# Adding a state's products on TensorE in two pieces instead of one, in the scan layers of a four-layer sequence model

## The reference

```
xz = h @ in_w;  xs, z = split(xz);  xs = silu(xs)
proj = xs @ xproj_w
dt = softplus(proj[..., :512] + dt_bias);  Bm, Cm = the next 64 and 64 columns
step:  hst = hst * exp(dt_t * A) + (dt_t * x_t) * B_t      # 512 channels x 64 states
       y_t = einsum('bds,bs->bd', hst, C_t)                # the sum over the states
y = ys + xs * Dskip
out = (y * silu(z)) @ out_w
```

## Time and profile before

| | |
|---|---|
| median of 3 runs | 4470.44 us (4468.05 to 4472.06) |
| the profiled execution | 4466.95 us |
| its span on the core | 4465.1 us |
| mean granted TensorE clock | 0.984 of full speed |
| scans of layer 1 | 295.0 to 1638 us |
| scans of layer 3 | 1948.7 to 4415.9 us |

### The profile page before, as it was taken

The page is one execution under the profiler, slowest core; times in us unless marked ns, Lnnn a source line. Parts: engine busy times, 40 slices in busy tenths (PEclk is TensorE's granted clock), DMA queues, the critical chain, the costliest instruction groups (busy, mean ns, idle before and its releaser), DMA issues.

```text
span 4465.1 us, 109964 instructions
## 1 busy us (share of the span) xinstructions
PE 4170.5 (93%) x45790; PEld 3234.7 (72%) x45790; DVE 4010.6 (90%) x3859; ACT 3863.4 (87%) x6050; POOL 3622.6 (81%) x1328
## 2 busy tenths in 40 slices
PE   9999899899899988989999999999999999999998
PEld 5457677677677764457877777778777777777777
DVE  6669999999999976669999999999999999999996
ACT  4569899899899964579999999999999999999995
POOL 3338898898888973349989998999998999888995
PEclk8999999999999999999999999999999999999999
DMA  4012121222122221032242422422422422323221
GB/s 167 1 29 67 58 65 62 57 60 67 58 59 67 69 73 41 1 53 72 85 78 79 86 70 76 83 74 82 84 75 68 87 82 94 62 79 70 72 83 40
DMA packets 241500, 305.18 MB, mean 68 GB/s; under 512 B 116448, under 2 KB 175712, under 8 KB 241008
## 3 DMA queue, kind: packets, MB, share of 16 engines
q1 hardware_dynamic: 241008, 298.15, 24.5%
HBM read 289.84 MB, written 8.26 MB: 67 GB/s over the span
## 4 chain that ended last, share of the span: by engine, by line
PE 41%; ACT 35%; DVE 16%; issue 7%; POOL 1%; DVEq 0%; DMA 0%; SPq 0%; POOLq 0%; ACTq 0%
PE psum L863 10%; ACT weights_c L1800 10%; PE psum L1152 8%; DVE work L2316 8%; PE psum L1134 8%; PE psum L1131 7%; ACT work L1817 6%; ACT work L1800 6%; ACT weights_c L1817 5%; PE psum L1279 5%; DVE weights_c L2316 4%; ACT L1498 2%; ACT modulation L1800 1%; PE psum L1362 1%; PE psum L1075 1%
## 5 line engine op out<-in xcount | busy, mean ns | idle before, releaser
L2739 POOL TENSOR_TENSOR work<-work,weights_a 128x2048 f32<-128x2048 f32 x512 | 1975.5, 3869 | 152.2 <-DVE work L2316 116.1
L2316 DVE TENSOR_TENSOR_SCAN work<-weights_c,psum 128x512 f32<-128x512 f32 x1316 | 1507.9, 1202 | 84.8 <-PE psum L1134 74.5
L2739 POOL TENSOR_TENSOR weights_c<-weights_c,weights_a 128x2048 f32<-128x2048 f32 x256 | 988.8, 3869 | 54.3 <-DVE weights_c L2316 52.8
L1134 PE MATMUL psum<-ident,work 128*128 128x128 f32 x5464 | 934.0, 273 | 0.0
L1800 ACT ACTIVATE work<-work,decay 128x504 f32<-128x504 f32 x1172 | 816.1, 707 | 72.0 <-DVE weights_c L2316 34.7
L2316 DVE TENSOR_TENSOR_SCAN weights_c<-work,psum 128x512 f32<-128x512 f32 x586 | 677.0, 1200 | 29.2 <-PE psum L1134 28.0
L2316 DVE TENSOR_TENSOR_SCAN work<-work,psum 128x512 f32<-128x512 f32 x586 | 675.7, 1200 | 28.5 <-PE psum L1134 26.8
L1134 PE MATMUL psum<-ident,weights_c 128*128 128x128 f32 x3752 | 696.9, 276 | 0.0
L1134 PEld LDWEIGHTS psum<-ident,work 128*128 128x128 f32 x5464 | 668.9, 142 | 0.0
L1152 PE MATMUL psum<-ident,work 64*128 64x64 f32 x16800 | 658.3, 229 | 10.2 <-POOL work L2739 8.1
L1152 PEld LDWEIGHTS psum<-ident,work 64*128 64x128 f32 x16800 | 586.0, 140 | 99.2 <-issue 74.4
(11 more groups left out here) (221 smaller groups left out, 6464.7 us busy)
## 6 DMA issues: line engine op xcount, KB each, us to landing
weights_a<-c_rows SPq DMA_DIRECT2D x384, 512.0 KB, 3.7
work<-b_diagonals SPq DMA_DIRECT2D x240, 128.0 KB, 2.2
weights_c<-b_diagonals SPq DMA_DIRECT2D x112, 128.0 KB, 2.1
b_diagonals<-weights_c SPq DMA_DIRECT2D x1, 4096.0 KB, 18.3
weights_c<-in_L_cond_fwd_in_w SPq DMA_DIRECT2D x8, 512.0 KB, 5.6
weights_c<-in_L_cond_fwd_xproj_w SPq DMA_DIRECT2D x4, 1024.0 KB, 7.2
weights_c<-in_L_cond_bwd_in_w SPq DMA_DIRECT2D x8, 512.0 KB, 5.4
weights_c<-in_L_cond_bwd_xproj_w SPq DMA_DIRECT2D x4, 1024.0 KB, 7.2
```

The source lines that it names most:

```text
L1134: last = nc.tensor.transpose(PS[:, bank, t * P:(t + 1) * P], buf["scaled"][s % INPUTS][t][:, j * P:(j + 1) * P], IDENT[:, :])
L2316: v.tensor_tensor_scan(buf["ring"][s % RING][:, along, j], buf["decay"][q % DECAYS[l]][:, along], PS[:, 4 + q % LOOKAHEAD, along], 0.0, AL ...
L2739: g.tensor_tensor(state, state, row.unsqueeze(2).broadcast_to([P, T, DC]), ALU.mult).then_inc(ss["prod_ready"], 1)
```

## The change

The add of a state is cut in two. Its turns 0 and 1 (16 transposes) come at PE's step 4s+9, and turns 2 and 3 (16 more) at step 4s+11. For the first state of a sum, these are 4s+11 and 4s+13. The wait for `half_turned` is now one wait at the second piece, for a semaphore that the first piece raised two steps earlier; the waits of `prod_ready`, `sum_done` of the state before, and of the first state's banks stand at the first piece. `sum_done` is raised by the second piece, at 4s+11 instead of 4s+10.

A piece of a projection or of another job that is due at a step which holds an add piece waits for the next step. Since adds are now at the odd steps, jobs go to the even ones. The skip term's add moves from step 22 (66) to 23 (67), stays in one place, and counts two increments of `skip_added` instead of one, for which the waits of ACT are adapted.

The instructions of DVE, ACT, POOL and SP stand in the same order as before.

```diff
-            step = s * DC + (11 if s % (states * together) == 0 else 10)
-            self.adds.setdefault(step, []).append(s)
+            step = s * DC + (11 if s % (states * together) == 0 else 9)
+            for half in range(2):
+                self.adds.setdefault(step + 2 * half, []).append((s, half))
...
-SKIPS = {1: (22, 66), 3: (22, 22)}
+SKIPS = {1: (23, 67), 3: (23, 23)}
...
-                def turn_by_rows(flat, begins, ends):
-
-                    nonlocal turns_done
-                    half, before = P // 2, turns_done
-                    for turn in range(TT):
-                        if turn >= 2:
-                            pe.wait_ge(ss["half_turned"], before + turn - 1)
+                def turn_by_rows(flat, turns, begins, ends):
+
+                    half = P // 2
+                    for turn in turns:
...
-                def add_up(s):
+                def add_up(s, half):
...
+                    flat = buf["ring"][s % RING].rearrange("p t j -> p (t j)")
+                    if half:
+                        pe.wait_ge(ss["half_turned"], s + 1)
+                        turn_by_rows(flat, (2, 3), begins, ends).then_inc(ss["sum_done"], 1)
+                        return
...
-                    turn_by_rows(flat, begins, ends).then_inc(ss["sum_done"], 1)
+                    turn_by_rows(flat, (0, 1), begins, ends).then_inc(ss["half_turned"], 1)
...
-                    for s in pl.adds.get(q, ()):
-                        add_up(s)
+                    for s, half in pl.adds.get(q, ()):
+                        add_up(s, half)
...
-                        while at is not None and (at <= step or step == pl.steps - 1):
+                        while at is not None and (at <= step and q not in pl.adds or step == pl.steps - 1):
```

More of the change, by code:

```diff
@@ L1136, in scan_input @@
                     last.then_inc(ss["input_ready"], 1)
-                turns_done = 0
-                def turn_by_rows(flat, begins, ends):
-                    nonlocal turns_done
-                    half, before = P // 2, turns_done
-                    for turn in range(TT):
-                        if turn >= 2:
-                            pe.wait_ge(ss["half_turned"], before + turn - 1)
+                def turn_by_rows(flat, turns, begins, ends):
+                    half = P // 2
+                    for turn in turns:
                         for k in range(DC):
@@ L1156, in turn_by_rows @@
                                                         tile_position=(g * half, 0))
-                        if turn < 2:
-                            last.then_inc(ss["half_turned"], 1)
-                            turns_done += 1
                     return last
-                def add_up(s):
+                def add_up(s, half):
                     r, n = divmod(s, pl.states)
                     begins, ends = s % (pl.states * pl.together) == 0, (s + 1) % (pl.states * pl.together) == 0
+                    flat = buf["ring"][s % RING].rearrange("p t j -> p (t j)")
[3 more added lines that the diff above has]
+                        return
                     if begins and r >= 1:
@@ L1171, in add_up @@
                         pe.wait_ge(ss["sum_done"], s)
-                    if n == SKIPS[l][r % 2] // DC - 1:
-                        pe.wait_ge(ss["skip_added"], r + 1)
-                    flat = buf["ring"][s % RING].rearrange("p t j -> p (t j)")
-                    turn_by_rows(flat, begins, ends).then_inc(ss["sum_done"], 1)
+                    if n == (SKIPS[l][r % 2] - 7) // DC:
+                        pe.wait_ge(ss["skip_added"], 2 * r + 2)
+                    turn_by_rows(flat, (0, 1), begins, ends).then_inc(ss["half_turned"], 1)
                 def add_skip(r):
-                    pe.wait_ge(ss["sum_done"], r * pl.states + (SKIPS[l][r % 2] - 6) // DC)
                     for i in range(2):
                         made("pool", f"skip{i}@{r}")
+                    pe.wait_ge(ss["sum_done"], r * pl.states + (SKIPS[l][r % 2] - 7) // DC)
                     flat = skip_at(l, r).rearrange("p j t -> p (j t)")
-                    turn_by_rows(flat, False, False).then_inc(ss["skip_added"], 1)
+                    turn_by_rows(flat, (0, 1), False, False).then_inc(ss["skip_added"], 1)
+                    pe.wait_ge(ss["skip_added"], 2 * r + 1)
+                    turn_by_rows(flat, (2, 3), False, False).then_inc(ss["skip_added"], 1)
                 yield from beside(-1)
@@ L1563, in steps_of @@
                         if l == 1 and j == 0:
-                            act.wait_ge(ss["skip_added"], r + 1)
+                            act.wait_ge(ss["skip_added"], 2 * r + 2)
                         f(buf["dt"][(r + 1) % 2][:, j, :], bank[f"dt{j}"], ACT.Identity,
```

## The result

The changed kernel takes 4554.51 us (median of 4, 4543.18 to 4556.49) against 4470.16 us before. The ratio is 1.0184 with a 95% interval of 1.0171 to 1.0198, so it is 84 us slower. Forecast was 4486 us, slower by 16, with a range up to 4528: the direction was right, the size was far off.

A forecast was written before the change was run, and what follows sets the result against it. No engine has much room (PE 93%, DVE 90% busy), and DVE waits for PE's bursts. Layer 3 +20, layer 1 -8, POOL +4 make +16 us: 4483 on the profiled execution, 4486 as median; own range 4480 to 4520, wider 4435 to 4528.

The forecast's parts named there:

- The price: PE's extra switch between whole and halved array: 0.30 us a state (ends 0 and 0.35), 230 us of PE time.
- Where the price is paid: Layer 3: a stretch grows only by the price its idle PE time doesn't cover; +20 us in all.
- The two full stretches of run 2: Layer 3: 8-state stretches with PE idle 0 and 0.42 us, expected to grow by 2.4 and 1.0 us.
- the third stretch in the earlier trace: Layer 3, PE idle 3.34 and DVE 2.27 us: better order can help, no growth, gain up to 1.9.
- hidden idle time: PE's waits show 0.16 us too short in the rows; some 6 a stretch give 1 us more room, except when full.
- Layer 1: Per run, full stretches lose 3.0 us and half the open ones' gain returns 2.1; taken as -1, so -8 us.
- The two full stretches of run 3: Layer 1, 4 states each, PE idle 0.27 and 0 us: expected to grow by 0.9 and 1.2 us.
- two open ones: Layer 1 stretches, PE idle 4.40 and 6.07 us: could win up to 2.8 and 3.2 us, half counted.
- POOL: First add piece needs POOL's product 1.2 us sooner; 132 waits, 44.9 us before; cost 0 to 158 us, taken as +4.
- That the even order wins: Rival: evened bursts let PE's and DVE's idle times cancel, price falls into PE idle time; 4431 us; faster had chance 0.27.
- POOL as the new bound: Rival: PE waits for POOL at step 4s+9 in full stretches; 4561 us; much slower cases had chance 0.07.
- The rival that every state with jobs pays in full: Waits don't shrink, some 600 states pay the whole price: 180 us, 4650 us; shares the 0.07 of the much slower cases.

The follow-up runs named there:

- switch-only kernel: Against the kernel before: add split but both halves kept at step 4s+10, around that step's input, jobs at all steps; 4543.46 us, ratio 1.0165.
- three switches at once: Against the split-only kernel: add in four pieces at steps 4s+9 to 4s+12, three more switches a state than before; 4865.35 us, ratio 1.0881.
- run 4: No follow-up kernel: one of layer 3's scan runs inside each execution; changed kernel against the one before, its third stretch went from 40.8 to 43.0 us.
- run 6: No follow-up kernel: one of layer 3's scan runs inside each execution; changed kernel against the one before, its third stretch went from 39.80 to 40.20 us.
- split-only kernel: Against the changed kernel: adds split the same way, but job pieces run when due, at add steps too; 4526.30 us, ratio 1.0122.
- Later readers: Against the changed kernel: every reader of a job's result on DVE, ACT and POOL placed one step later; 4545.46 us, ratio 1.0169.
- jobs-only one: Against the kernel before: add whole at 4s+10, job pieces due at an add's step wait for the next; 4458.99 us, ratio 0.9973.
- jobs-only one with later readers: Against the kernel before: whole add, job pieces kept off its step, every reader of job results one step later; 4470.55 us, ratio 1.0003.
- two whole-array kernels: Against the kernel before: state adds as 16 transposes of 128x128, no switch; together 4609.66 us, or spread over four steps 4540.34 us.
- later readers in one layer: Against the kernel before: whole add, job pieces kept off its step and readers one step later, in layer 3 alone; 4453.05 us, ratio 0.9957.

## Why the prediction was wrong

**The price was right.** I took 0.30 us a state from bounds of 0 and 0.35. The changed trace shows 0.31, the full stretch of the switch-only kernel 0.31, and three switches at once 0.27 each. The reading of the idle time was right in kind, too: full stretches grow, those without jobs don't.

**The step that failed is "Where the price is paid", in layer 3.** I put it at +20 us; it was +62 us. Of PE's idle time I had assumed that it takes up most of the price: 154 us of price (512 states), 20 left over. The starts of PE's matmuls show that its waits ahead of inputs in layer 3 fell from about 192 to 105 us. So some 87 us of the price of 159 us (at 0.31) were taken up, and what is left, about 70, is near the 62 of the length. By runs:

| runs of layer 3 | forecast | measured |
|---|---|---|
| 2, 4, 6 | +12 | +10.8, +10.1, +8.1 |
| 0, 1, 3, 5 | +8 | +3.2, +7.9, +9.9, +9.1 |
| 7 | 0 | +3.0 |

Four things were wrong in the working or left out of it:

- I averaged PE's idle time over too long stretches, 8 states in run 2 and a whole run of 64 in the others (306.0 us against 309.7 in run 3). DVE holds two full banks, 2.2 us, about half a state, so idle time of PE in one state can pay for little beyond the next. A sum over the trace before bears this out: take the measured price, 0.31 us a state, less PE's waits ahead of inputs, in each stretch where something is left. Over stretches of 64 states that leaves 2 us of growth for layer 3, over 8 states 40, over 2 states 65, over single states 75; measured were 62. For layer 1 the same sums are 0, 13, 20 and 28 us; measured were 24. The totals fit one or two states; single stretches scatter too much to show it one by one. The two full stretches of run 2 grew by 2.0 and 2.1 us where I had 2.4 and 1.0.
- I counted the third stretch in the earlier trace rows (2721.10 to 2761.90, both engines idle) as a gain of up to 1.9 us. It grew by 2.2. Its idle time was mostly one wait, and the trace before shows it: PE waited for ACT's scaled input (L1817) once, for 2.5 us (2.8 in the weight load's row), which I had not looked up. ACT was busy with jobs and two table loads just then. A single long wait of PE for a third engine is no room for the price elsewhere, and no order of PE's own work cancels it. PE before, then after:

```profile
2730.38 0.49 PE L1131 MATMUL psum<-work 128*128 128x128 f32 x2 [2.51 <-ACT work L1817]
```

```profile
2770.40 0.79 PE L1132 MATMUL psum<-work 128*128 128x128 f32 x2 [2.19 <-ACT work L1816]
```

- The growth of 2.2 us in that stretch isn't the price, though. Its granted clock fell to 0.96 in the mean, in run 4 as well, where it also went from 40.8 to 43.0 us. In run 6 the clock stayed at 1.00, and the stretch grew by 0.4. So most of the 2.2 us seem to go with the lower clock (see the last section). This is no clean separation, since the wait for ACT was shorter in run 6 as well, 1.3 us before and 1.0 after. Run 6 before, then after:

```profile
3965.90:4005.70 39.80, 37.56 (x434) 30.08 (x432) 38.48 (x38) 39.10 (x58) 33.90 (x11) 1.00 0.24 82
```

```profile
4044.90:4085.10 40.20, 39.06 (x438) 30.84 (x437) 38.45 (x37) 38.58 (x58) 33.88 (x11) 1.00 0.25 82
```

- I added hidden idle time, 1 us a stretch, to PE's room. By the starts of the matmuls it was 0.3 to 0.9 us. The stretch before the last grew by 2.7 us where I had 0, and the price of 8 states is 2.5. There was also a longer wait in it: a job piece of PE (L864) waited 1.2 us for ACT, against 0.2 before.

Two smaller slips carry no weight. DVE's scan takes 1.11 us from start to start (71.1 us for 64), not 1.14. And the two stretches that I called the first two of run 2 are its first and its third.

**Layer 1: -8 forecast, +24 measured.** The two full stretches of run 3 grew by 2.3 and 2.3 us instead of 0.9 and 1.2. In the switch-only kernel they have 25.2 and 24.6 us:

```profile
899.10:924.30 25.20, 24.93 (x259) 17.80 (x258) 20.71 (x20) 21.88 (x37) 20.02 (x7) 1.00 0.15 53
924.30:948.90 24.60, 24.60 (x248) 17.79 (x249) 21.13 (x21) 23.37 (x35) 19.55 (x7) 1.00 0.18 58
```

That is 1.2 us more each, the price of 4 states as forecast. The other 1.1 us in each came with moving adds and jobs about. Of the two open ones, one grew by 1.1 and the other shrank by 2.0, where I had counted on 2.8 and 3.2 of gain at most. Here too the granted clock moved, from 1.00 and 0.88 to 0.94 in both, so their difference isn't the order's alone. DVE's waits for job results rose: its gated product waited 12.7 us instead of 1.0. With the split alone layer 1 has 1356.3 us, with the job rule 1366.9, so about 13 us came with the split and 11 with the rule. (The traced execution of the split-only kernel took 4536.16 us, 10 above its median, so this division is a rough one.) Later readers made it worse (1375.0), so it is not simply that DVE comes too early. In that kernel and in the jobs-only one with later readers, DVE's waits in layer 1 moved from its jobs to its scans. What else the rule does in layer 1 stays open; the pieces that fall together at the even steps, two at a time, would be one reason, which wasn't tested.

**POOL: +4 forecast, nothing measured.** The add's waits for POOL fell although the first piece stands a step earlier. After (answers to the earlier trace rows):

```profile
  POOL work L2738: 15.3, 33
...
  POOL weights_c L2738: 7.7, 10
```

That is 23.0 us instead of 44.9. PE is later than before, so the product is there.

**The sum as the runs give it.** The switch alone costs +72 us. Evening out by the split gives back 17, and the job rule at two steps of four costs 28. These add up to the 84 measured because each is the difference of two neighbouring kernels, so the sum is no check of its own; that each step alone is clear of noise is what it rests on. The rivals stand as follows. That the even order wins is refuted in this kernel, but the mechanism exists: 69 us between the two whole-array kernels, 13 us for the jobs-only one. POOL as the new bound is refuted. The rival that every state with jobs pays in full (+180 us) was 96 us off on the other side, my forecast 68. About a third of the price, 84 of 238 us (768 states at 0.31), is the growth of the whole. With three switches a state it is 394 of 622 us (at 0.27), as PE's idle time is used up.

## What to carry to other kernels

Where two engines run at 93% and 90% of the span, time added to one can be lost in good part, here a third of a small dose and nearly two thirds of three times as much. Idle time seems to pay for it only near the place where it lies, as far as the buffers between the engines reach, here two banks or 2.2 us. Average spare time over stretches little longer than that, and look first whether the spare time is one long wait for a third engine. Where lengths of single stretches are compared, compare their granted clocks too. Spread a burst only if cutting it costs little: in this kernel cutting one into two for 0.3 us a state lost 55 us net, while moving other work out of its way, at no price, won 13 and with later readers in one layer 18.

## What the runs showed of the hardware

- A switch of PE from matmuls on the whole array to pairs on its halves and back costs 0.27 to 0.31 us here (three measurements above). The Trainium skill, "TensorEngine Tiling (Array Packing)", section Tiling Modes, says that changing the tiling mode drains TensorE. The runs agree that the change costs time, and put the number beside it.
- A scan of DVE that nothing holds up starts 1.11 us after the one before, while its own record lasts 1.20 us. So each wait costs the overlap of 0.09 us beside the idle time that the row shows. DVE's busy time rose by 40 us (4010.6 to 4050.6) with the same instructions. The 257 more waits for PE's inputs at 0.09 us each are 23 us of it. The mean record of a scan also grew, from 1201 to 1205 ns, 14 us in all, for which no reason was found. So here many short waits cost more than few long ones of the same sum.
- After the wait of PE for ACT, 2.2 us, the granted clock in the changed kernel was 0.57 of full speed from 2770 to 2774 us (so mostly at 1.2 GHz), and 16 small transposes took 1.12 us instead of 0.71. After a wait of 2.5 us at the same place the kernel before stayed at 1.00. Both kernels have a mean clock near 0.98, so over the whole this explains little. In this stretch of 8 states it goes with a growth of 2.2 us; in run 6, where PE waited 1.0 us at that place and the clock stayed at 1.00, the growth was 0.4.

```profile
2771.76 1.12 PE L1148 MATMUL psum<-ident,weights_c 64*128 64x64 f32 x16
```

```profile
2770.00:2774.00 4.00, 3.60 (x27) 3.16 (x28) 2.28 (x2) 4.00 (x8) 3.78 (x2) 0.57 0.02 4
```
